# The expert weights of a mixture-of-experts decoder layer, asked for by GpSimd in its own DMA queue

## The chip, the core and the metric

The kernel runs on one core of one Trainium2 chip. The time is the device time of one execution in microseconds, as the median of several runs. All data are 32-bit floats.

## What is computed

Three blocks follow one another, each with a layer norm ahead and a residual addition behind: windowed attention, a long convolution against a context, and a feed-forward block. Only the last touches the change. It has a shared part and 64 experts; each of the 2048 tokens goes to 6 of them, and an expert takes at most 128:

```python
xd = zeros(E, CAP + 1, D).at[e_flat, slot].set(x[tok])        # E 64, CAP 128, D 512
h = square(relu(einsum('ecd,eid->eci', xd, w1)))              # I 256
yd = einsum('eci,edi->ecd', h, w2)
routed = zeros(T, D).at[tok].add(yd[e_flat, slot] * gate)     # T 2048
out = x + square(relu(x @ su.T)) @ sd.T + routed
```

## The kernel before

The kernel is written engine by engine, with semaphores between the engines. The attention and the convolution end at about 480 us; the router and the shared part follow, and from about 550 us to the end the kernel is the loop over experts.

For each expert four things move. The load brings its weights, 128 rows of 8 KB, 1 MB, from HBM into one of 8 slots (`wring`, four slots of their own, two in the upper half of the residual tile `X`, two below `xg`). The gather (`gather`, L592) brings the 128 token rows of 2304 B that the router chose, out of `token_rows` in HBM, into one of 8 slots of `xg`. TensorE transposes them (`tokens_T`, L1652), multiplies by the first weights (`hidden`, L1659) and by the second (`outputs`, L1669). VectorE scales the result by the gates into one of NY = 4 slots of `ysb` and writes the row numbers for GpSimd (L1334 to L1336). The scatter (`scatter`, L598) adds these 128 rows of 2 KB into `out` in HBM. Two experts may hold the same token, so a scatter waits until the one before has landed (`pool.wait_ge(added, before)`). After every 15 scatters of a group of 16, one scatter of 256 KB more (`scatter_tiles`, L611) adds a tile of the shared part, which TensorE computes between the experts; it stands in the same chain.

GpSimd's order for slot n is: wait for VectorE's rows, wait for scatter n-1 to land, scatter n, a product on one column (`begun_mark`, L609) that raises `scatter_begun`, gather n+8. The product stands behind the scatter on GpSimd and so tells SyncE that the scatter's descriptors have been written.

SyncE holds the loads (L414 to L434). Load n+6 waits for `scatter_begun` to pass n+1; the slot that it fills was last read by expert n-2. The first six loads wait for nothing of this kind: they follow the write of the gates (L413), the fifth and sixth also the write of the upper result rows (`upper_written`, L420). Between loads six and seven SyncE writes the lower result rows to HBM in three parts (L422 to L426), on which the first scatter waits.

SyncE's and ScalarE's transfers run in hardware queues (q1 and q10 in the profile), GpSimd's in a software queue (q0).

Of the kernel before, what the change touches and what calls it, by code (L numbers as in the profile page):

```python
# [6 lines left out]
P = 128  # L7
B, S, D = 8, 256, 512
T = B * S
# [10 lines left out]
E, K, NG, TKG, CAP, I = 64, 6, 8, 4, 128, 256  # L20
# [41 lines left out]
def program(nc, a, out):  # L62
    f32, u32 = mybir.dt.float32, mybir.dt.uint32
    ALU, ACT, AX = mybir.AluOpType, mybir.ActivationFunctionType, mybir.AxisListType
    V, G, A, TE = nc.vector, nc.gpsimd, nc.scalar, nc.tensor
    ds = bass.ds
# [6 lines left out]
    with ctx:  # L73
        def sb(name, shape, dt=f32):
            return ctx.enter_context(nc.sbuf_tensor(name, shape, dt))

        def sem(name):
            return ctx.enter_context(nc.semaphore(name))


        X = sb("residual", [P, NT, D])
# [9 lines left out]
        minus_half = sb("minus_half", [P, NT])  # L91
# [6 lines left out]
        idxs = sb("scatter_rows", [P, 4], u32)  # L98
        idxt = sb("tile_scatter_rows", [P, 1], u32)
        tile_rows = sb("tile_rows", [P, NT // 4])  # L100
        begun_mark = sb("begun_mark", [P, 1])
        AREA = 34400
        arena = sb("arena", [P, AREA])
        place = [0]
# [61 lines left out]
        NW, AHEAD = 8, 6  # L166
# [32 lines left out]
        UE, NY = 8, 4  # L199
# [18 lines left out]
        empt = [sem(f"bank{k}_drained") for k in range(NBANK)]  # L218
# [51 lines left out]
        tile_ready = sem("shared_tile_ready")  # L270
        added = sem("rows_added_to_the_result")
        scatter_landed = sem("scatter_landed")
        scatter_begun = sem("scatter_descriptors_written")
        out_written = sem("result_rows_begun")
        upper_written = sem("upper_result_rows_begun")

# [75 lines left out]
        FS = Fills(FC.after, names)  # L352
# [7 lines left out]
        @block.sync  # L360
        def _(sp):
            for u in range(4):
                sp.dma_start(X[:, u, :], a["x"][u * P:(u + 1) * P, :]).then_inc(tile_loaded[u], 16)

            def load(dst, name, s):
                sp.dma_start(dst, a[name]).then_inc(s, 16)

            load(wq, "wq", w_loaded)
            load(wkv, "wkv", w_loaded)
            load(rope, "rope", tables_loaded)  # L370
            load(bias, "bias", tables_loaded)
            load(bo, "bo", tables_loaded)
            load(wo, "wo", tables_loaded)
            load(kpad[:, P:], "kern", small_loaded)
            load(dcol[:], "skip", small_loaded)

            for s in (*empt, *conv_used, *conv_filled, *y_filled, *y_ready, hsq_ready, tile_ready):
                sp.sem_inc(s, 1)
            sp.sem_inc(scatter_landed, 5)
            sp.sem_inc(conv_done, 2)  # L380

            sp.wait_ge(tables_loaded, 16 * 4)
            for i in range(1, PAIRS):
                if i > 1:
                    sp.wait_ge(x_loaded, i * 16 - 16)
                sp.dma_start(X[:, i * 4:i * 4 + 4, :],
                             a["x"][i * (4 * P):(i + 1) * (4 * P), :].rearrange("(t p) d -> p t d", p=P)).then_inc(x_loaded, 16)

            sp.wait_ge(consts_ready, 1)
            sp.dma_start(out[T:ROWS, :], zeros[:]).then_inc(zero_written, 16)  # L390
            sp.dma_start(xrows[T:ROWS, 0:D], zeros[:]).then_inc(zero_written, 16)
            sp.dma_start(xrows[T:ROWS, D:XW], zeros[:, 0:E]).then_inc(zero_written, 16)
            sp.wait_ge(pad_ready, 1)
            sp.dma_start(toep[:], kpad[:]).then_inc(toep_written, 16)

            sp.wait_ge(full[FA1.bank(("vmid",))], FA1.filled(("vmid",)))
            sp.wait_ge(toep_written, 16)
            toep_v = bass.AP(toep.tensor, 1, [[P + D, SH], [1, P], [1, D]])
            with sp.Fori(0, SH // NTR) as i:
                for s in range(NTR):  # L400

                    sp.wait_ge(conv_filled[s], i + 1)
                    sp.wait_ge(toep_written, 16)
                    sp.dma_start(tring[:, s:s + 1, :], toep_v[ds(i * NTR + s, 1), :, :].rearrange("h p d -> p h d"))\
                      .then_inc(head_loaded[s], 16)
                    sp.dma_start(cring[:, s, :, :].rearrange("p m i -> p (m i)"),
                                 a["ctxE"][ds((i * NTR + s) * P, P), :]).then_inc(head_loaded[s], 16)

            for k, t in enumerate(TILES3):
                sp.wait_ge(x3_ready[k % NX], k // NX + 1)  # L410
                sp.dma_start(xrows[t * P:(t + 1) * P, 0:D], x3[:, k % NX, :]).then_inc(x3_written[k % NX], 16)
            sp.wait_ge(gates_ready, 1)
            sp.dma_start(xrows[0:T, D:XW].rearrange("(t p) c -> p t c", p=P), W).then_inc(gates_written, 16)  # L413
            def load_expert(s, i):  # L414
                sp.dma_start(wring[s], a["wexp"][ds((i * UE + s) * P, P), :]).then_inc(wexp_loaded[s], 16)

            for s in range(UE):
                if s == 4:

                    sp.wait_ge(upper_written, 16)  # L420
                if s == 6:
                    for first, last in ((0, 3), (4, 6), (7, 7)):  # L422
                        name = ("dn", last // 4, last % 4)
                        sp.wait_ge(empt[FS.bank(name)], FS.drained(name))
                        sp.dma_start(out[0:T, :].rearrange("(t p) d -> p t d", p=P)[:, first:last + 1, :],
                                     X[:, first:last + 1, :]).then_inc(out_written, 16)  # L426
                if s >= AHEAD:
                    sp.wait_ge(scatter_begun, s - AHEAD + 1)
                load_expert(s, 0)
            with sp.Fori(1, E // UE) as i:  # L430
                for s in range(UE):

                    sp.wait_ge(scatter_begun, i * UE + (s - AHEAD + 1))
                    load_expert(s, i)  # L434

            sp.wait_ge(added, 16 * (E + NT // 4))

# [2 lines left out]
        def _(pool):  # L440
# [142 lines left out]
            G.drain()  # L583
            G.tensor_scalar(W, W, 2.5, None, ALU.mult).then_inc(gates_ready, 1)

            for k in range(NX):
                pool.wait_ge(x3_written[k], 16 * (NT // NX))
            pool.wait_ge(gates_written, 16)
# [9 lines left out]
            def scatter(s, i, before):  # L598

                pool.wait_ge(y_ready[s % NY], i * (UE // NY) + (s // NY + 2))  # L600
                if before is not None:
                    pool.wait_ge(added, before)
                    pool.sem_inc(scatter_landed, 1)
                pool.indirect_dma_start(out, bass.IndirectOffsetOnAxis(ap=idxs[:, s % NY:s % NY + 1], axis=0),  # L604
                                        ysb[:, s % NY, :], None, compute_op=ALU.add).then_inc(added, 16)

                if before is not None:
                    pool.wait_ge(scatter_begun, i * UE + s)
                G.tensor_tensor(begun_mark[:], minus_half[:, 0:1], minus_half[:, 0:1], ALU.mult).then_inc(scatter_begun, 1)  # L609

            def scatter_tiles(j):  # L611
                pool.wait_ge(tile_ready, j + 2)
# [1174 lines left out]
```

## Time and profile before

| | us |
|---|---|
| median of 3 runs | 976.17 |
| lowest and highest | 974.54, 979.42 |
| the profiled execution | 984.94 |
| its span | 982.7 |
| TensorE busy | 895.9 |
| VectorE busy | 552.3 |
| GpSimd busy | 462.6 |
| ScalarE busy | 232.2 |
| moved by DMA | 143.40 MB |

The profiled execution is 8.8 us longer than the median. Its own time is 2.2 us more than its span. Times in the trace count from the span's start. "Busy" of GpSimd at a transfer is the time in which it writes the transfer's descriptors, not the time in which data move; the idle time in brackets stands ahead of an instruction, with what ended it. The shares of a DMA queue are the time that its packets took, over 16 engines and the stretch asked for. A link of the chain of scatters, as the word is used below, is the time from the start of one scatter on GpSimd to the start of the next.

### The profile page before, as it was taken

How to read it: one execution, taken by the hardware profiler on the slowest of the kernel's cores; microseconds unless marked ns; L12 is line 12 of the kernel's file. 1: busy time of each engine (PE TensorE's matmuls, PEld its weight loads, DVE VectorE, ACT ScalarE, POOL GpSimd, SP SyncE). 2: the span in 40 equal slices, each digit the busy share in tenths (PEclk: the TensorE clock that was granted, in tenths of full speed). 3: DMA queues.
4: the chain of work that ended last, by engine and by line, in shares of the span. 5: the costliest groups of instructions: out<-in, count | busy, mean ns of one | idle time of the engine just before them, and what ended most of it. 6: DMA issues, size and time to landing. Idle time of an engine off the chain costs nothing. (4 is left out here: it accounts for less than half of the span.)

```text
span 982.7 us, 14587 instructions
## 1 busy us (share of the span) xinstructions
PE 895.9 (91%) x4941; PEld 624.8 (64%) x4941; DVE 552.3 (56%) x1145; ACT 232.2 (24%) x715; POOL 462.6 (47%) x513
## 2 busy tenths in 40 slices
PE   5899999998999999999999999999999899989880
PEld 3666666665777777775444586867766667675640
DVE  4787888878688888977888323222222222212220
ACT  1555656462300000122100021211111111111110
POOL 1644352536488888620271344444444444444432
PEclk9989999999999999999999999999999999999995
DMA  7300000020633333042007568988898898888863
GB/s 293 113 1 2 1 2 1 2 76 1 236 93 93 93 94 93 1 150 108 1 1 275 180 197 259 268 257 225 254 274 261 226 265 254 261 241 247 236 148 53
DMA packets 44190, 143.40 MB, mean 146 GB/s; under 512 B 7345, under 2 KB 11697, under 8 KB 35185
## 3 DMA queue, kind: packets, MB, share of 16 engines
q1 hardware_dynamic: 27472, 98.56, 27.3%
q0 software_dynamic: 14912, 37.76, 19.6%
q10 hardware_dynamic: 1760, 6.49, 1.7%
q8 instruction: 27, 0.44, 0.2%
q14 instruction: 19, 0.15, 0.0%
HBM read 114.36 MB, written 28.43 MB: 145 GB/s over the span
## 5 line engine op out<-in xcount | busy, mean ns | idle before, releaser
L1375 PE MATMUL ps<-arena 128*128 128x128 f32 (+4 forms) x2112 | 511.2, 400 | 9.3 <-DVE arena L817 5.7
L1375 PEld LDWEIGHTS ps<-arena 128*128 128x128 f32 x2112 | 336.9, 191 | 146.6 <-issue 101.7
L604 POOL DMA_INDIRECT out<-arena,scatter_rows x64 | 101.2, 1581 | 219.0 <-DMA out<-arena,scatter_rows 145.4
L1309 DVE TENSOR_TENSOR arena<-arena 128x256 f32<-128x256 f32 x64 | 27.5, 430 | 219.8 <-ACT arena L802 213.5
L1375 PE MATMUL ps<-features_T,arena 128*128 (+2 forms) x640 | 116.0, 338 | 0.0
L1375 PEld LDWEIGHTS ps<-features_T,arena 128*128 128x128 f32 x640 | 84.7, 188 | 37.3 <-issue 37.3
L654 ACT ACTIVATE arena<-ps 128x512 f32<-128x512 f32 (+1 forms) x136 | 78.1, 591 | 117.5 <-PE ps L1656 49.0
L475 POOL TENSOR_TENSOR arena<-arena 128x512 f32<-128x512 f32 x48 | 49.3, 1060 | 89.6 <-DVE arena L837 89.6
L802 ACT ACTIVATE arena<-ps 128x256 f32<-128x256 f32 x64 | 24.6, 384 | 257.9 <-PE ps L1375 249.7
L593 POOL DMA_INDIRECT arena<-token_rows,gather_rows x64 | 66.1, 1034 | 38.2 <-DVE gather_rows L1302 27.1
L664 ACT ACTIVATE arena<-arena 128x128 f32<-128x128 f32 x192 | 74.0, 388 | 17.2 <-DVE arena L825 17.2
L528 POOL TENSOR_TENSOR arena<-arena 128x512 f32<-128x512 f32 x32 | 40.7, 1273 | 47.1 <-DVE arena L1094 47.1
L1656 PEld LDWEIGHTS ps<-ident,arena 128*128 128x128 f32 x256 | 30.1, 140 | 49.8 <-DMA arena<-token_rows,gather_rows 33.2
L1694 PE MATMUL ps<-arena 128*128 128x512 f32 x128 | 57.5, 592 | 0.0
L1656 PE MATMUL ps<-ident,arena 128*128 128x128 f32 x256 | 39.2, 276 | 20.1 <-DMA arena<-token_rows,gather_rows 20.1
L1334 DVE COPY scatter_rows<-slot_rows_u 128x1 uint32 (+1 forms) x64 | 9.8, 154 | 71.6 <-PE ps L1375 56.4
L609 POOL TENSOR_TENSOR begun_mark<-minus_half 128x1 f32<-128x1 f32 x64 | 50.0, 781 | 0.0
L1336 DVE TENSOR_SCALAR arena<-ps,arena 128x512 f32<-128x512 f32 x64 | 47.9, 748 | 0.0
L1694 PEld LDWEIGHTS ps<-arena 128*128 128x128 f32 x128 | 24.3, 190 | 30.6 <-issue 30.6
L765 ACT ACTIVATE arena<-features_T 128x256 f32 x32 | 13.0, 416 | 122.0 <-DVE arena L1094 120.2
L1101 DVE TENSOR_REDUCE arena<-arena 128x1024 f32 (+1 forms) x32 | 38.7, 1208 | 0.0
L664 ACT ACTIVATION_READ_ACCUMULATOR arena<-arena 128x1 f32 x192 | 36.1, 188 | 0.0
(178 smaller groups left out, 1086.8 us busy)
## 6 DMA issues: line engine op xcount, KB each, us to landing
arena<-wexp SPq DMA_DIRECT2D x48, 1024.0 KB
residual<-wexp SPq DMA_DIRECT2D x16, 1024.0 KB
arena<-toeplitz_rows SPq DMA_DIRECT2D x32, 256.0 KB, 3.1
arena<-ctxE SPq DMA_DIRECT2D x32, 192.0 KB, 3.2
token_rows<-arena SPq DMA_DIRECT2D x16, 256.0 KB, 2.4
residual<-x SPq DMA_DIRECT2D x3, 1024.0 KB, 5.3
arena<-suT ACTq DMA_DIRECT2D x1, 2048.0 KB, 7.7
arena<-sdT ACTq DMA_DIRECT2D x1, 2048.0 KB, 12.4
```

The lines of the kernel that those rows point to most:

```text
L475: G.tensor_tensor(e, e, rinv[:, b, 4 * c:4 * c + 4, q:q + 1].broadcast_to((P, 4, P)), ALU.mult)\
L528: G.tensor_tensor(halfsum[:, s % 2].rearrange("p m j k -> p (m j) k"), pv[:, :, 0:4], pv[:, :, 4:8], ALU.add).then_inc(half_ready, 1)
L593: pool.indirect_dma_start(xg[:, s, :], None, xrows, bass.IndirectOffsetOnAxis(ap=idxg[:, s:s + 1], axis=0))\
L604: pool.indirect_dma_start(out, bass.IndirectOffsetOnAxis(ap=idxs[:, s % NY:s % NY + 1], axis=0), ysb[:, s % NY, :], None, compute_op=ALU.a ...
L609: G.tensor_tensor(begun_mark[:], minus_half[:, 0:1], minus_half[:, 0:1], ALU.mult).then_inc(scatter_begun, 1)
L654: A.activation(dst, src, ACT.Copy, **kw).then_inc(empt[bank], 1)
L664: ins = A.activation(prob[:, b, k, q, :], prob[:, b, k, q, :], ACT.Exp, bias=negmax[:, b, k, q:q + 1], scale=1.0, accum_out=rowsum[:, b, k ...
L1101: V.tensor_reduce(o[:, 0:2 * B, :], prodb[:, s % 2, 0:2 * B], axis=AX.X, op=ALU.add)
L1336: V.tensor_scalar(ysb[:, s % NY, :], ps[:, 4 + s % 2, :], xg[:, s, ds(i * UE + (D + s), 1)], None, ALU.mult)\
L1375: ins = TE.matmul(out_ap, lhsT, rhs, start=(n == 0), stop=(n == len(pairs) - 1))
L1656: ins = TE.transpose(ps[:, bank, c * P:(c + 1) * P], xg[:, s, c * P:(c + 1) * P], ident[:])
L1694: ins = TE.matmul(ps[:, 7, :], htile[:, k, :], sdT[:, k, :], start=(k == 0), stop=(k == 7))
```

## The change

GpSimd issues the loads. The helper `load_expert` moves from SyncE to GpSimd, with the slot and the expert's number as arguments. GpSimd issues the first AHEAD = 6 loads after the last product on the gates and before it waits for the row numbers, with the wait on `upper_written` ahead of the fifth. After that, load n+6 follows scatter n directly and stands ahead of gather n+8. The one-column product, its tile, the semaphore `scatter_begun`, the wait on it and SyncE's loop are gone. SyncE keeps the three writes of the lower result rows. Slots, sizes, lead and the waits of all other engines stay.

```diff
@@ sync
-            def load_expert(s, i):
-                sp.dma_start(wring[s], a["wexp"][ds((i * UE + s) * P, P), :]).then_inc(wexp_loaded[s], 16)
-
-            for s in range(UE):
-                if s == 4:
-
-                    sp.wait_ge(upper_written, 16)
-                if s == 6:
-                    for first, last in ((0, 3), (4, 6), (7, 7)):
-                        name = ("dn", last // 4, last % 4)
-                        sp.wait_ge(empt[FS.bank(name)], FS.drained(name))
-                        sp.dma_start(out[0:T, :].rearrange("(t p) d -> p t d", p=P)[:, first:last + 1, :],
-                                     X[:, first:last + 1, :]).then_inc(out_written, 16)
-                if s >= AHEAD:
-                    sp.wait_ge(scatter_begun, s - AHEAD + 1)
-                load_expert(s, 0)
-            with sp.Fori(1, E // UE) as i:
-                for s in range(UE):
-
-                    sp.wait_ge(scatter_begun, i * UE + (s - AHEAD + 1))
-                    load_expert(s, i)
+
+            for first, last in ((0, 3), (4, 6), (7, 7)):
+                name = ("dn", last // 4, last % 4)
+                sp.wait_ge(empt[FS.bank(name)], FS.drained(name))
+                sp.dma_start(out[0:T, :].rearrange("(t p) d -> p t d", p=P)[:, first:last + 1, :],
+                             X[:, first:last + 1, :]).then_inc(out_written, 16)
@@ gpsimd, behind the last product on the gates
+            def load_expert(slot, ahead):
+                pool.dma_start(wring[slot], a["wexp"][ds(ahead * P, P), :]).then_inc(wexp_loaded[slot], 16)
+
+            for s in range(AHEAD):
+                if s == 4:
+                    pool.wait_ge(upper_written, 16)
+                load_expert(s, s)
+
@@ gpsimd, scatter(s, i, before)
-                if before is not None:
-                    pool.wait_ge(scatter_begun, i * UE + s)
-                G.tensor_tensor(begun_mark[:], minus_half[:, 0:1], minus_half[:, 0:1], ALU.mult).then_inc(scatter_begun, 1)
+                if not isinstance(i, int) or i * UE + s + AHEAD < E:
+                    load_expert((s + AHEAD) % UE, i * UE + (s + AHEAD))
```

## Rows read from the trace of the kernel before

**Rows 1.** Stages: stretch, length, busy us by engine, TensorE's clock, DMA share, GB/s.

```profile
569.00:636.00 67.00, 67.00 (x419) 51.30 (x418) 18.60 (x49) 13.02 (x28) 32.28 (x35) 1.00 0.86 255
636.00:955.00 319.00, 297.90 (x1694) 213.94 (x1692) 83.29 (x227) 50.94 (x111) 141.19 (x147) 0.99 0.85 244
```

**Rows 2.** Waits, 560 to 960 us: who waited for what, us, times, longest.

```profile
POOL out L604 <- DMA out<-arena,scatter_rows: 141.6, 46, 6.9
PEld ps L1656 <- DMA arena<-token_rows,gather_rows: 33.2, 20, 4.4
POOL out L604 <- DVE arena L1336: 20.8, 4, 11.2
```

**Rows 3.** Timeline of GpSimd, links of the chain of scatters: start, length, instruction, idle before.

```profile
633.93 1.58 POOL L604 DMA_INDIRECT out<-arena,scatter_rows  x1 [2.28 <-DMA out<-arena,scatter_rows]
...
643.85 1.58 POOL L604 DMA_INDIRECT out<-arena,scatter_rows  x1 [6.93 <-DMA out<-arena,scatter_rows]
644.88 0.77 POOL L609 TENSOR_TENSOR begun_mark<-minus_half 128x1 f32<-128x1 f32 x1
645.81 1.04 POOL L593 DMA_INDIRECT arena<-token_rows,gather_rows  x1 [0.16 <-issue]
649.24 1.58 POOL L604 DMA_INDIRECT out<-arena,scatter_rows  x1 [2.38 <-DMA out<-arena,scatter_rows]
...
930.99 1.58 POOL L604 DMA_INDIRECT out<-arena,scatter_rows  x1 [6.85 <-issue]
...
947.40 1.56 POOL L604 DMA_INDIRECT out<-arena,scatter_rows  x1 [3.76 <-DMA out<-arena,scatter_rows]
...
952.82 1.56 POOL L604 DMA_INDIRECT out<-arena,scatter_rows  x1 [3.55 <-DMA out<-arena,scatter_rows]
...
969.44 1.56 POOL L615 DMA_INDIRECT out<-arena,tile_scatter_rows  x1 [3.70 <-DMA out<-arena,scatter_rows]
976.25 1.55 POOL L604 DMA_INDIRECT out<-arena,scatter_rows  x1 [5.25 <-issue]
```

**Rows 4.** By line: VectorE's scaling, L1336, ns and first and last; scatters, L604, to landing.

```profile
L1336 DVE TENSOR_SCALAR arena<-ps,arena x64: 740/750/752, 567.7 to 955.3; 128x512 f32<-128x512 f32 x64
...
DMA to landing us min/median/max: 4.5/4.8/9.1
```

**Rows 5.** DMA queues in 649.24:654.79, 633.93:643.85, 947:969, 580:933, 550:557, in that order.

```profile
q0 software_dynamic: 224, 0.56, 50.1%
q1 hardware_dynamic: 147, 1.07, 46.3%
...
q1 hardware_dynamic: 252, 1.81, 47.8%
q0 software_dynamic: 303, 0.85, 38.3%
...
q0 software_dynamic: 576, 1.05, 37.9%
...
q0 software_dynamic: 12608, 31.96, 45.2%
q1 hardware_dynamic: 7865, 57.22, 41.3%
...
q0 software_dynamic: 372, 1.39, 75.5%
```

**Rows 6.** SyncE's issues of the loads: ns min/median/max, first and last.

```profile
L415 SPq DMA_DIRECT2D arena<-wexp x48: 332/333/1387, 521.5 to 938.4; - x48
```

**Rows 7.** GpSimd by line, 580 to 933 us: busy us, mean ns, idle before.

```profile
L593 POOL DMA_INDIRECT arena<-token_rows,gather_rows x55 | 57.2, 1041 | 8.8 <-issue 8.8
```

**Rows 8.** Timelines of GpSimd and of SyncE's queue at the loop's start.

```profile
518.30 2.80 POOL L584 TENSOR_SCALAR arena<-arena 128x1024 f32<-128x1024 f32 x1 [0.16 <-issue]
548.17 1.23 POOL L593 DMA_INDIRECT arena<-token_rows,gather_rows  x1 [27.07 <-DVE gather_rows L1302]
525.25 0.99 SPq L415 DMA_DIRECT2D residual<-wexp  x2
```

More of the change, by code:

```diff
@@ L100, in program @@
         tile_rows = sb("tile_rows", [P, NT // 4])
-        begun_mark = sb("begun_mark", [P, 1])
         AREA = 34400
@@ L272, in program @@
         scatter_landed = sem("scatter_landed")
-        scatter_begun = sem("scatter_descriptors_written")
         out_written = sem("result_rows_begun")
```

## The prediction

> **What bounds the kernel now.** I read the stages first, then the waits, then the single links of the chain. TensorE's busy share of the whole (895.9 of 982.7 us) names TensorE, but is an average. The table by stage [rows 1] splits the mixture-of-experts loop: from 569 to 636 us TensorE never stops, from 636 to 955 us it is busy 297.90 of 319.00 us, so it lacks 21.1 us; after 955 us the last scatters go on for 28 us without it. The waits [rows 2] say what it lacks: gathered token rows. The same table says what GpSimd, which asks for those rows, waits for: 141.6 us in 46 waits for its own last scatter to land, and 20.8 us in 4 waits for rows from VectorE. So from about 636 us the bound is a chain on GpSimd: a scatter-add may start only when the one before has landed. 64 expert scatters and 4 tile scatters make 67 links from 569.34 to 976.25 us, 406.9 us, 6.07 each.
>
> The timeline of GpSimd [rows 3] gives the link. Undisturbed it takes 643.85 to 649.24 = 5.39 us. Near the end, when no weights and no token rows are moved, it is the same: 947.40 to 952.82 = 5.42. A tile scatter makes 6.81. So 5.45 is the latency of one link and not a share of bandwidth, and the floor of the chain is 63 x 5.45 + 4 x 6.8 = 370.6 us. TensorE's own floor: the 64 products reach VectorE from 567.7 to 955.3 us [rows 4], 387.6 us, less the 21.1 us of idle: 366.5. The two nearly coincide, and the chain has 406.9 - 370.6 = 36.3 us above its floor. The longest links hold half of that. Five take more than 8 us; the first of them is 633.93 to 643.85 = 9.92 us, the last ends at 930.99 us after an idle time of 6.85 where an undisturbed link has 2.4 [rows 3]. Together they take 45.3 us against 27.3, 18 us of excess.
>
> What fills a long link is in the DMA table. In the link 649.24 to 654.79, near the floor, the transfers of q0 (GpSimd's) take 50.1% of the 16 engines and those of q1 (weights) 46.3%; in the long one q1 has 252 packets against 147 and 47.8%, beside q0's 38.3% [rows 5]; a scatter lands after 4.8 us in the median and 9.1 at most [rows 4]. Packets of the weights that were asked for after this scatter move while it is still unfinished.
>
> **What the change removes, adds and moves.** (1) SyncE's loop goes: its waits and issues of 333 ns [rows 6]. SyncE has nothing else to do there; worth nothing.
>
> (2) The one-column product goes with its wait: 0.77 us busy [rows 3]. In a link [rows 3] the scatter issues at 0, the product at 1.03, the gather at 1.96, and GpSimd is free at 3.00, then idle for 2.4 us until the landing. So it is hidden: nothing on the path.
>
> (3) In its place GpSimd issues the load, 128 rows of 8 KB. No row shows a plain transfer from GpSimd. The nearest are the gather, 128 rows in 1041 ns [rows 7], and the start of the product 1.03 us behind the scatter [rows 3]. From below: SyncE's 333 ns. From above: the scatter writes 128 pieces of 2 KB in 1.03 us; if a load's rows were cut to 2 KB too, it would be 512 pieces, 4.2 us. I take 1.04, the nearest in kind, plus an estimated 0.1 for the steps that form the address. The gather then starts at 1.03 + 1.14 = 2.2 instead of 1.96 and GpSimd is free at 3.2; the next scatter is due at 5.4. Cover 2.2 us: the sum is zero up to a load cost of about 3.4 us and each us above that is 1 us per link.
>
> (4) The start of the loop: GpSimd now asks for six loads after its last gate product, which ends at 521.1, and then waits for the row numbers until 548.17, 27 us idle [rows 8]. Six times 1.14 us fit. SyncE gave loads five and six out at 525.25 [rows 8], so the wait on the upper rows' write that now stands on GpSimd was over by then; behind it in the queue are only waits that end at 548. Nothing. SyncE's three writes of result rows wait for nothing new.
>
> (5) The order of the transfers. This is where the time can move. Today q0 holds scatter n, gather n, scatter n+1, and q1 the loads; on an engine that is late they share. Now one queue holds scatter n, load n, gather n, scatter n+1. The work of each, from [rows 5]: four scatters alone take 37.9% of 22 us, 2.08 us each on all engines; in 580 to 933 us q1's 57.22 MB, 54.6 loads, take 41.3% of 353 us, 2.67 us each; q0's 45.2% is 159.6 us, less 55 x 2.08 and three tile scatters of twice that, leaves 32.7 us, 0.6 per gather. Sum 5.35 us, against a link of 5.45: it just fits. The link 649.24 to 654.79 has 50.1% + 46.3% [rows 5], so there is a little room and no more. Load n is ready directly behind scatter n instead of after GpSimd's mark, SyncE's wake-up and issue, and fills it earlier.
>
> The gain: in a long link the late engine must no longer carry load n (2.67 us) and its share of gather n before it finishes scatter n; it must carry what was left of load n-1, which it carries now too. I take 2.0 us of the 3.6 us excess of each of the five long links, 10 us, and 0.05 us of each of some 45 other expert links after 636 us, 2 us: 12 us. Not more, because the same stall holds every engine in either order, and because up to 636 us TensorE sets the pace. TensorE lacks 21.1 us, so it can follow the 12. 982.7 - 12 = 970.7 for the span, 973 for this execution's 984.94. The median of the runs shown is 976.17, 8.8 us less than the profiled execution, so the excess without the profiler is about 27 instead of 36 us; the gain scales to 9: **967 us**.
>
> The Trainium skill (DMA: Bandwidth & Descriptors, Queues, rings and completion order) says that each engine takes turns between queues packet by packet, and works off one queue in order. That is the mechanism behind the gain, and the long link's two shares [rows 5] agree.
>
> **The rivals.** *A, the forecast:* 967, own range 955 to 974.
>
> *B, no change:* the long links come from stalls that hold all packets alike, so order is worth nothing. For it: in the long link q0 and q1 together fill 86% of the engines against 96% in the good one [rows 5], so part of it is no question of turns. Against: q1's extra packets in it. 976, range 972 to 980.
>
> *C, slower:* loads can no longer be put off. Today they have six experts of lead and the scatter takes its turn beside what is left of them; in one queue scatter n+1 stands behind all of load n and gather n. It decides where the work of a link exceeds 5.45 us, and I have 5.35, on an edge: 10% on a load (2.94) already gives 5.6. I price it at 0.35 us per link on the 50 links after 636 us, +17: 993. For it: the DMA shares are near full, and six gathers right after one another in 550 to 557 us, 1.39 MB, took 75.5% of 7 us, 3.8 us for a MB where q1 needs 2.55 [rows 5]; a load at that price is 4.0 us, a link 6.7. Against: that stretch starts on idle engines. Between scatters a gather comes out at 0.6 us for 0.29 MB, about q1's rate, and a load will stand behind a scatter in the same way. So I keep 2.67 for the forecast and 0.35 for C.
>
> *D, issue cost:* the load costs 4.2 us on GpSimd (512 pieces); 0.8 above the cover on 60 links, +50: 1026. Against: 64 gathers of 128 rows at 1041 ns.
>
> *E, slow transfers from GpSimd:* a load moves at the rate of all that q0 moves. 159.6 us for 31.96 MB [rows 5] is 5.0 us for a MB, 5.2 a load; a link is then 2.08 + 5.2 + 0.6 = 7.9, 1.8 above today's 6.07 on some 58 links, +105: 1081. Against: the scatters are most of those 159.6 us, and a scatter both reads and adds. The Trainium skill (DMA: Bandwidth & Descriptors, Bandwidth) gives 6.15 us for a 1 MB load issued from GpSimd; by that the kernel would end near 1135. Its section SWDGE vs HWDGE vs iDMA has plain transfers issued from SyncE or ScalarE, a rule against this change. No row here shows a load from GpSimd.
>
> **How the numbers follow.** A 0.42, B 0.20, C 0.25, D 0.07, E 0.06. Faster or slower by over 0.5% (4.9 us, about what a measurement of this kernel can tell from no change) means below 971.3 or above 981.1. A gives 0.40 of faster and 0.02 of same; B 0.02 of faster, 0.16 of same, 0.02 of slower; C 0.04 of same and 0.21 of slower; D and E slower. Faster 0.42, same 0.22, slower 0.36. The range leaves out D, E and the outer tails of A and C, together under 0.2: 952 to 1000. Both signs are well populated, so A's own range, 955 to 974, is the one to read beside it.
>
> **What the profile of the changed kernel would show.** Right: links over 8 us gone or under 7.5; undisturbed links at 5.4 to 5.5; the load's instruction near 1.0 us on GpSimd and still over 1.5 us of idle before each scatter; TensorE's waits for gathers below 10 us; hardly any traffic on q1 after 570 us. C would show undisturbed links of 5.7 and more, with a scatter that lands after more than 5.0 us. D would show GpSimd's scatter waiting for issue and not for a landing; E a link near 8 us. The prediction fails most easily if a load from GpSimd takes the engines longer than q1's 2.67 us, since the sum 5.35 has 0.1 us to spare.

## The result, and the profile after

The changed kernel takes 1007.53 us in the median of 4 runs (1006.98 to 1009.09), the kernel before 977.79 us beside it. The ratio on record is 1.0315, 95% interval 1.0274 to 1.0356 (the two medians alone give 1.0304): about 30 us slower, where 9 us faster was forecast. The profiled execution took 1006.98 us with a span of 1004.9 us. Of the four runs of e13 below, two were in a slower state of the chip, and its time and ratio are those of the two fast ones.

The first view is the table by stage of the changed kernel; its columns are those of [rows 1].

```profile
569.00:636.00 67.00, 67.00 (x424) 51.86 (x424) 19.04 (x50) 12.84 (x28) 32.66 (x30) 1.00 0.84 235
636.00:955.00 319.00, 287.03 (x1619) 212.81 (x1618) 77.96 (x213) 48.96 (x107) 158.30 (x145) 0.95 0.86 241
955.00:1005.00 50.00, 19.35 (x83) 11.32 (x81) 6.12 (x18) 2.14 (x6) 13.12 (x9) 0.73 0.45 76
```

Up to 636 us nothing has changed for TensorE: it never stops. From 636 to 955 us it lacks 32.0 us where it lacked 21.1 [rows 1], and it still has 19.35 us of work after 955 us, where it had none. The DMA engines are as full as before (0.86 against 0.85) but move 241 GB/s against 244. TensorE's granted clock falls as well, from 0.99 to 0.95, in the stretch in which it has more idle time.

The waits from 560 to 990 us say for what, and are the rows that answer [rows 2]:

```profile
POOL out L595 <- DMA out<-arena,scatter_rows: 141.2, 49, 4.6
PEld ps L1646 <- DMA arena<-token_rows,gather_rows: 40.1, 19, 6.2
PE ps L1646 <- DMA arena<-token_rows,gather_rows: 32.0, 13, 6.0
POOL out L595 <- DVE arena L1326: 11.4, 1, 11.4
```

The bound is the same chain. GpSimd waits for a scatter to land and hardly ever for data: VectorE's rows are waited for once instead of four times, 11.4 us instead of 20.8, so it isn't a slower TensorE or VectorE that holds the chain up. The 67 links now run from 570.46 to 995.33 us, 424.9 instead of 406.9 us. The profiled executions differ by 22 us, 18 of them in the chain; that of the kernel before was itself 7 us above its median, so the medians differ by 30.

The timeline of GpSimd shows two kinds of link, the answer to [rows 3]. (Start, length, instruction; the idle time ahead of it in brackets.)

```profile
703.61 1.62 POOL L595 DMA_INDIRECT out<-arena,scatter_rows  x1 [3.87 <-DMA out<-arena,scatter_rows]
704.63 1.21 POOL L570 DMA_DIRECT2D arena<-wexp  x1
709.24 1.62 POOL L595 DMA_INDIRECT out<-arena,scatter_rows  x1 [2.09 <-DMA out<-arena,scatter_rows]
710.26 1.22 POOL L570 DMA_DIRECT2D arena<-wexp  x1
716.74 1.62 POOL L595 DMA_INDIRECT out<-arena,scatter_rows  x1 [3.95 <-DMA out<-arena,scatter_rows]
```

The load stands 1.02 us behind the scatter and takes 1.21 us; GpSimd is idle for 2.1 us even in the short link (5.63 us) and for almost 4 us in the long one (7.50). Taking the difference of each two scatter starts in this view: the median of the 63 links that start with an expert scatter is 5.86 us, before it was 5.64. Among them links over 8 us went from 5 to 2 (8.17 and 8.13), but links over 6.5 us went from 11 to 20. The five very long ones were traded for many of 7 to 7.8 us, 14 instead of 1. (Of the four links behind tile scatters, one grew from 6.65 to 8.66 us.)

By line, the scatters and the loads of the changed kernel, and under each the time from issue to landing (compare [rows 4] for the scatters):

```profile
L595 POOL DMA_INDIRECT out<-arena,scatter_rows x64: 1551/1617/2130, 570.5 to 995.3; - x64
...
DMA to landing us min/median/max: 4.6/5.0/7.4
...
L570 POOL DMA_DIRECT2D arena<-wexp x48: 550/1211/1250, 522.2 to 956.0; - x48
...
DMA to landing us min/median/max: 6.4/8.8/18.1
```

The DMA queues tell the rest. First both kernels in the same stretch, 650 to 900 us (q0 and q1 of the kernel before, then q0 of the changed one), then loads alone: the kernel before in 530 to 538 us and the changed one in 528 to 534 us. Columns: packets, MB, share of the 16 engines.

```profile
q0 software_dynamic: 9000, 22.98, 46.4%
q1 hardware_dynamic: 5501, 39.96, 40.3%
```

```profile
q0 software_dynamic: 13653, 59.30, 85.5%
```

```profile
q1 hardware_dynamic: 479, 3.43, 101.8%
```

```profile
q0 software_dynamic: 361, 2.58, 101.9%
```

Alone, loads from GpSimd are as quick as loads from SyncE: 1.019 x 6 us / 2.58 MB = 2.37 us for a MB, and 1.018 x 8 / 3.43 = 2.37. Between scatters and gathers they are not. Before, the packets took 0.867 x 250 / 62.94 MB = 3.44 us of all engines for a MB; after, 0.855 x 250 / 59.30 = 3.60 us. An expert moves 1.64 MB (load 1.05, gather 0.29, scatter 0.26, its part of the tile 0.03), so its packets take 5.91 instead of 5.64 us. I call this the packet time of an expert below. (The prediction's sum of 5.35 us is the same quantity without the tile scatters, which it left out.) It is made of the times that packets take, so a packet that only waits in its engine counts too. It is therefore partly an effect of the order of the transfers and not a pure price of the load: the experiments give it between 5.68 and 6.13 us with the same whole loads from GpSimd.

### The profile page after: what moved, and what is told of

It is laid out like the page before. It is cut to its first block and busy times, and to the rows that moved or that the text cites. A ratio compares the mean times of both kernels' runs of the same rounds, so it can differ in the third digit from the quotient of the medians.

```text
span 1004.9 us, 14411 instructions
## 1 busy us (share of the span) xinstructions
PE 903.9 (90%) x4941; PEld 634.4 (63%) x4941; DVE 552.1 (55%) x1145; ACT 232.1 (23%) x715; POOL 489.3 (49%) x513
## 5 line engine op out<-in xcount | busy, mean ns | idle before, releaser
L1365 PE MATMUL ps<-arena 128*128 128x128 f32 (+4 forms) x2112 | 519.8, 406 | 8.7 <-DVE arena L807 5.7
L1365 PEld LDWEIGHTS ps<-arena 128*128 128x128 f32 x2112 | 345.3, 197 | 146.0 <-issue 101.3
L595 POOL DMA_INDIRECT out<-arena,scatter_rows x64 | 103.7, 1621 | 204.9 <-DMA out<-arena,scatter_rows 141.2
L584 POOL DMA_INDIRECT arena<-token_rows,gather_rows x64 | 65.8, 1028 | 42.4 <-DVE gather_rows L1292 23.6
L1646 PE MATMUL ps<-ident,arena 128*128 128x128 f32 x256 | 41.4, 287 | 32.0 <-DMA arena<-token_rows,gather_rows 32.0
L1646 PEld LDWEIGHTS ps<-ident,arena 128*128 128x128 f32 x256 | 31.8, 146 | 60.6 <-DMA arena<-token_rows,gather_rows 40.1
L570 POOL DMA_DIRECT2D arena<-wexp x48 | 55.8, 1162 | 0.0
L1684 PEld LDWEIGHTS ps<-arena 128*128 128x128 f32 x128 | 24.4, 191 | 30.5 <-issue 30.5
```

The costliest lines, as they stand in the source:

```text
L570: pool.dma_start(wring[slot], a["wexp"][ds(ahead * P, P), :]).then_inc(wexp_loaded[slot], 16)
L584: pool.indirect_dma_start(xg[:, s, :], None, xrows, bass.IndirectOffsetOnAxis(ap=idxg[:, s:s + 1], axis=0))\
L1365: ins = TE.matmul(out_ap, lhsT, rhs, start=(n == 0), stop=(n == len(pairs) - 1))
L1646: ins = TE.transpose(ps[:, bank, c * P:(c + 1) * P], xg[:, s, c * P:(c + 1) * P], ident[:])
L1684: ins = TE.matmul(ps[:, 7, :], htile[:, k, :], sdT[:, k, :], start=(k == 0), stop=(k == 7))
```

## The experiments

Three theories stand against one another. **W**: what the packets of an expert take on the engines sets the time, and loads from GpSimd take more. **Q**: the single queue has a price of its own, because a scatter stands behind everything that was put in before it. **P**: GpSimd's own time for issuing the loads is what costs. G, S and "sharing" name smaller rivals where they come up. "Packet time" is worked out for each run as above, from its DMA queues in 650 to 900 us. For cut loads the MB of an expert are fewer. "Chain" is the time from the first scatter to the last in the profiled execution. The ratio compares with runs of the kernel before from the same series, whose medians lie between 976.4 and 982.8 us; it is the ratio on record and need not be the quotient of two medians.

| kernel | total us | ratio to before (95%) | chain us | packet time us |
|---|---|---|---|---|
| before | 977.79 | | 406.9 | 5.64 |
| changed | 1007.53 | 1.0315 (1.0274 to 1.0356) | 424.9 | 5.91 |
| e1 gather ahead of load | 1013.32 | 1.036 (1.0296 to 1.0424) | 432.7 | 6.13 |
| e2 load ahead of scatter | 1071.47 | 1.0955 (1.087 to 1.1039) | 490.7 | 5.68 |
| e3 changed, half loads | 963.14 | 0.9847 (0.9774 to 0.9921) | 382.8 | 4.72 |
| e4 before, half loads | 959.11 | 0.9806 (0.9731 to 0.9881) | 381.5 | 4.46 |
| e5 loads from both | 1019.52 | 1.0431 (1.0342 to 1.052) | 438.0 | 5.93 |
| e6 before, loads in two parts | 991.62 | 1.0144 (1.006 to 1.0228) | 413.4 | 5.91 |
| e7 load after landing | 1018.92 | 1.0399 (1.0296 to 1.0502) | 438.8 | 5.74 |
| e8 changed, product back | 1008.28 | 1.0291 (1.0194 to 1.0388) | 429.5 | 5.98 |
| e9 changed, 1856 columns | 992.17 | 1.0154 (1.0101 to 1.0207) | 412.4 | 5.71 |
| e10 before, 1856 columns | 967.93 | 0.9928 (0.989 to 0.9966) | 386.7 | 5.39 |
| e11 changed, 1664 columns | 979.15 | 1.0025 (0.9991 to 1.0059) | 395.8 | 5.43 |
| e12 before, 1664 columns | 963.58 | 0.9868 (0.9803 to 0.9933) | 386.8 | 5.20 |
| e13 pairs from SyncE | 1036.04 | 1.056 (quotient of the medians) | 458.6 | 5.48 |
| e14 pairs from GpSimd | 1083.65 | 1.1026 (1.0988 to 1.1065) | 503.8 | 5.83 |

### Is it the bytes in the queue, or the issue on GpSimd? Half the load (e3, e4)

```diff
- pool.dma_start(wring[slot], a["wexp"][ds(ahead * P, P), :])
+ pool.dma_start(wring[slot][:, 0:1024], a["wexp"][ds(ahead * P, P), 0:1024])
```

(e4 has the same edit in SyncE's loop. The first six loads stay whole.)

> The changed kernel whose loads from the seventh on bring only the first 4 KB of each row, the first part of the first weights; the rest of the slot keeps the weights of an earlier expert. GpSimd issues as many loads as before. Theory Q: the queue's work per link falls from about 5.5 to 4.2 us, below the latency of 5.45, so the links go to 5.4 to 5.5 us, none but a few above 6.5, and TensorE becomes the bound: total 950 to 962. Theory P (issue or path): the number of loads and their issue are the same, so the links stay above 5.7 and the total above 990.

> The kernel before with the same halved loads from the seventh on, from SyncE. Theory Q: with half the bytes neither order has a full engine, so it comes to the same time as the changed kernel with halved loads within 5 us, 950 to 962. Theory P: it is ahead of it by about the 25 us that separate the two full kernels.

Measured: 963.1 and 959.1 us, 4 us apart as Q has it, with e3 1 us above its range. The median link is 5.60 us in e3 and 5.58 in e4, and TensorE is busy 290 and 289 of the 294 us from 636 to 930, so it sets part of the pace now. The number of loads is the same as in the full kernels, the issue of a half load on GpSimd takes 1.21 us like that of a whole one, and the gap falls from 30 to 4 us. P, with links above 5.7 us and a total above 990, is out: what costs goes with the bytes. The engines are no longer full; q0 of e3 in 650 to 900 us:

```profile
q0 software_dynamic: 15510, 45.89, 77.8%
```

The packet time of an expert is 4.72 us in e3 and 4.46 in e4. The surplus of loads from GpSimd, 0.26 us, is there in full, just as with whole loads (0.27), but it costs nearly nothing: a link of 5.45 us has room for it. In these runs packet time counts only where it comes near the latency of a link.

### Is issuing really covered? (e8)

```diff
+ G.tensor_tensor(begun_mark[:], minus_half[:, 0:1], minus_half[:, 0:1], ALU.mult).then_inc(scatter_begun, 1)
  if not isinstance(i, int) or i * UE + s + AHEAD < E:
      load_expert((s + AHEAD) % UE, i * UE + (s + AHEAD))
```

> The changed kernel with the one-column product and its wait back between the scatter and the load: GpSimd's own work per link grows by 0.8 to 0.9 us. Theory Q: GpSimd is idle for over 2 us ahead of each scatter, so the issue is hidden; the load and the gather reach the queue 0.9 us later, which costs nothing as long as the scatter still moves then: 1007 within 6 us. Theory P (GpSimd's issue time is the cost): 0.8 us per link more, 1050.

Measured 1008.3 us, no change. (Its profiled execution has a chain 4.7 us longer than the changed kernel's, a median link of 6.17 us and 26 links over 6.5. Counts of links in one execution can differ that much between kernels of equal time.) The run tests less than it was meant to: the timeline shows the load starting while the product runs.

```profile
704.48 1.62 POOL L597 DMA_INDIRECT out<-arena,scatter_rows  x1 [1.94 <-DMA out<-arena,scatter_rows]
705.52 0.80 POOL L602 TENSOR_TENSOR begun_mark<-minus_half 128x1 f32<-128x1 f32 x1
705.66 1.22 POOL L572 DMA_DIRECT2D arena<-wexp  x1
707.17 1.03 POOL L586 DMA_INDIRECT arena<-token_rows,gather_rows  x1 [0.30 <-issue]
711.96 1.63 POOL L597 DMA_INDIRECT out<-arena,scatter_rows  x1 [3.76 <-DMA out<-arena,scatter_rows]
```

The gather starts 2.69 us behind the scatter; in the changed kernel the load alone puts it at 2.5. So GpSimd's work grew by about 0.2 us and not by 0.8 to 0.9. The result agrees with a hidden issue; the proof of that is in e3.

### Do late gathers cost? (e1)

```diff
# in outline
  scatter(n)
- load(n + 6)
  gather(n + 8)
+ load(n + 6)
```

> The changed kernel with gather and load in the other order: scatter n, gather n+8, load n+6. Theory Q (one queue: a scatter waits for all that was put into the queue before it, so every delay of a load reaches the chain): load and gather both still stand ahead of the next scatter, so the chain keeps its time, 424.9 us for 67 links within 6 us, and the total stays near 1007; TensorE's waits for gathers get shorter by a few us because the gathers land up to 2.7 us sooner. Theory G (the loss comes from gathers that land late behind the loads, and the chain only follows TensorE): the total returns to 980 to 990.

Measured 1013.3 us, a little more than the changed kernel. TensorE's waits, 560 to 1000 us:

```profile
PE ps L1371 <- issue: 27.9, 20, 3.5
PEld ps L1652 <- DMA arena<-token_rows,gather_rows: 10.2, 5, 3.2
PE ps L1652 <- DMA arena<-token_rows,gather_rows: 8.4, 3, 3.0
```

The waits for gathers fall from 32.0 and 40.1 us to 8.4 and 10.2, and the time does not fall at all; the idle time turns up at the products instead (27.9 us, where the kernel waits for a free row buffer or bank). G is refuted: gathers that land sooner don't bring the time back. Q was right about the gathers and a little off on the chain: 432.7 us where 424.9 within 6 was expected. The packet time rises too, to 6.13 us, with nothing but the order changed. Why the order gather, load is slightly worse was not settled.

### What a load directly ahead costs, in the same queue and in another (e2, e7)

```diff
  pool.wait_ge(added, before)
+ load_expert((s + AHEAD) % UE, i * UE + (s + AHEAD))        # e2
  pool.indirect_dma_start(out, ..., compute_op=ALU.add).then_inc(added, 16)
- load_expert((s + AHEAD) % UE, i * UE + (s + AHEAD))
```

```diff
- sp.wait_ge(scatter_begun, i * UE + (s - AHEAD + 1))        # e7, SyncE, from the kernel before
+ sp.wait_ge(added, 16 * (n + n // GROUP))                   # n = expert - AHEAD + 1
```

> The changed kernel with load n+6 issued directly ahead of scatter n, behind the wait for the landing of scatter n-1. Theory Q: the scatter now stands behind a whole fresh load, so a link grows from about 5.8 by the load's 2.7 us of transfer to 8 to 8.5 us, the total to 1140 to 1180. Theory P (what costs is the issue of the load on GpSimd, 1.2 us, and not the queue): a link grows by the issue alone, 1.2 us, total about 1080. If order in the queue meant nothing and issue were hidden: 1007.

> The kernel before without the one-column product: SyncE gives out load n+6 when scatter n has landed, about 3 us later than before, so that its packets move together with those of scatter n+1 in another queue. Theory Q: even then the two queues share, and a link stays shorter than in the run with the load directly ahead of the scatter in one queue (7.45 us): 6 to 6.8 us, total 985 to 1030. If sharing between queues gave the scatter nothing, 7.2 us or more and 1050 or more. If the time of the load did not matter at all: 978.

Measured: e2 1071.5 us, e7 1018.9 us. The link of e2, from its timeline:

```profile
652.28 0.56 POOL L570 DMA_DIRECT2D arena<-wexp  x1 [3.64 <-DMA out<-arena,scatter_rows]
653.14 1.63 POOL L597 DMA_INDIRECT out<-arena,scatter_rows  x1 [0.31 <-issue]
655.07 1.01 POOL L584 DMA_INDIRECT arena<-token_rows,gather_rows  x1 [0.30 <-issue]
659.72 0.57 POOL L570 DMA_DIRECT2D arena<-wexp  x1 [3.63 <-DMA out<-arena,scatter_rows]
660.59 1.63 POOL L597 DMA_INDIRECT out<-arena,scatter_rows  x1 [0.30 <-issue]
```

A link is 7.45 us: 0.87 us of issue ahead of the scatter, and a landing after 5.9 us in the median instead of 5.0. Q had 8 to 8.5 us and 1140 to 1180 in total and is too high; it counted the whole load. P's 1080 is nearer, and rightly so here: ahead of the scatter the issue can't be hidden and makes 0.87 of the 1.6 us by which the link grew. That Q's part is smaller than a load may come from the load starting to move before the scatter's own packets are ready, which no view here shows. e7 came out where Q had it: a link of 6.5 us, 1019 us in total. Its landing takes 5.7 us (e2 first):

```profile
DMA to landing us min/median/max: 4.5/5.9/7.3
```

```profile
DMA to landing us min/median/max: 4.5/5.7/7.5
```

In e7 SyncE gives the load out 0.77 us ahead of the scatter (at 653.85 us, the scatter starts at 654.62), in e2 GpSimd does so 0.86 us ahead; in the kernel before it is 1.98 us behind. So at about the same lead a load in another queue holds a scatter up almost as long as one in the scatter's own queue, and the difference of the two totals is mostly the 0.87 us of issue. A second queue is weaker protection than I had taken it for. What counts here is how much of a load has been given out when the scatter comes.

### How much is packet time, how much the single queue? (e6, e9 to e12)

e6 gives the kernel before the packet time of the changed one by other means: SyncE asks for each load in two parts. (TensorE's wait on the load, not shown, counts both.)

```diff
- sp.dma_start(wring[s], a["wexp"][ds((i * UE + s) * P, P), :]).then_inc(wexp_loaded[s], 16)
+ for h in (0, 1024):
+     sp.dma_start(wring[s][:, h:h + 1024], a["wexp"][ds((i * UE + s) * P, P), h:h + 1024]).then_inc(wexp_loaded[s], 16)
```

> The kernel before with each load as two transfers from SyncE of 128 rows of 4 KB, one after the other, both behind the same product. Theory Q with turns taken between the two queues: smaller packets of the loads give the scatter its turn sooner on an engine that is late, so the links above 6.5 us get shorter, total 968 to 976. If turns do not matter: 978 within 4 us; if the larger number of packets costs: 980 to 985.

Measured 991.6 us, ratio 1.0144: 14 us slower, above all three expected ranges. My hope that finer packets give the scatter its turn sooner is refuted; it became a control instead. Its queues in 650 to 900 us:

```profile
q0 software_dynamic: 8731, 22.24, 45.0%
q1 hardware_dynamic: 10650, 38.77, 43.0%
```

0.88 x 250 / 61.01 MB = 3.61 us for a MB, 5.91 us for an expert, the same as the changed kernel, with the loads still in SyncE's queue. At this packet time SyncE's queue gives 1.0144 and GpSimd's 1.0315.

The other way round, the loads of both kernels are cut by 9% and by 19%:

```diff
- pool.dma_start(wring[slot], a["wexp"][ds(ahead * P, P), :])
+ pool.dma_start(wring[slot][:, 0:1856], a["wexp"][ds(ahead * P, P), 0:1856])     # e9; e11: 1664
```

> The changed kernel whose loads from the seventh on bring 1856 of 2048 columns of each row, 9% less; the last columns of the second weights stay those of an earlier expert. Theory W (a load from GpSimd costs the 16 engines some 0.25 us more per expert, 3.6 against 3.4 us for a MB of all traffic, and the engines are full): 9% of a load is 0.25 us, so it comes back to the kernel before, 974 to 982. Theory Q (the single queue has a price of its own, because the scatter cannot take its turn when an engine is late): it stays above, 984 to 996.

> The kernel before with the same cut of the loads, from SyncE. The engines are at their limit in the kernel before too, so 0.25 us less work per link gives 0.15 to 0.25 us per link back: 964 to 970. If the kernel before had slack in its engines: 976 to 980, no change.

> The changed kernel with loads of 1664 of 2048 columns, 19% less. Theory W: the time of the kernel before with 1856 columns, 964 to 970. Theory Q: 970 to 980, since the engines are late less often but the order still costs when they are.

> The kernel before with loads of 1664 of 2048 columns. Both theories: near the floor that halved loads gave (959), 958 to 965.

Measured: 992.2, 967.9, 979.2 and 963.6 us. The queues in 650 to 900 us, e9 and then e10:

```profile
q0 software_dynamic: 14154, 57.82, 85.8%
```

```profile
q0 software_dynamic: 9479, 24.17, 49.6%
q1 hardware_dynamic: 5808, 38.25, 37.8%
```

Q's ranges hold in e9 and e11, W's in neither; e10 and e12 came out as expected. The gap between the two kernels goes 30, 24, 16, 4 us with 2048, 1856, 1664 and 1024 columns. Two pairs stand at nearly the same packet time: e9 (5.71) has 992 us and the kernel before (5.64) 977.8; e11 (5.43) has 979.2 and e10 (5.39) 967.9. From before to e10, 0.25 us of packet time are 7 us by the ratio and 10 by the medians, so the small differences explain 3 and 2 us at most of the 14 and 11. Some 9 to 11 us stay with the single queue there. At full size it is about 17, by 1.0315 against 1.0144; with intervals of 0.4% and 0.8% that is 17 within about 9. The rest of the 30 us, about 13, goes with the packet time. Both theories are needed, and the runs can't fix their shares closely. That the two parts simply add is an assumption. So is their being separate: with whole loads from GpSimd the packet time is 5.68 us in e2, 5.91 in the changed kernel, 5.98 in e8 and 6.13 in e1, so the order moves it as well.

The cut of the kernel before is also worth a look: 9% fewer bytes in the loads gave 0.7% of the time, twice as much cut gave 1.3%. Some of the time of the kernel before goes with the bytes already.

### A longer burst ahead of every second scatter (e13, e14)

```diff
+ wpair = [wfixed[:, 0:2, :], wfixed[:, 2:4, :], whigh, wlow]
- sp.dma_start(wring[s], a["wexp"][ds((i * UE + s) * P, P), :]).then_inc(wexp_loaded[s], 16)
+ sp.dma_start(wpair[s // 2], a["wexp"][ds((i * UE + s) * P, 2 * P), :].rearrange("(k p) n -> p k n", p=P))
+   .then_inc(wexp_loaded[s], 16)                              # even s alone; e14 the same from GpSimd
```

(TensorE waits for the load of the pair, not shown.)

> The kernel before with one transfer of 2 MB for two experts, given out by SyncE after every even scatter; the slots allow it. Same bytes, half as many load transfers. Theory W (what the engines work per MB sets the time): half the transfers cost less, some 3.37 us for a MB instead of 3.44; if the engines stay as full, 966 to 974. Theory Q (order): the second half of the 5.3 us burst moves together with the next scatter, from another queue, so it delays it by less than its own length: odd links 6.5 to 7, even ones 5.4, total 975 to 995.

> The changed kernel with one transfer of 2 MB for two experts, given out by GpSimd behind every even scatter. Theory W alone: fewer transfers, so it gains on the changed kernel as the SyncE version gains on the kernel before, 995 to 1003, and the two pair versions lie 25 to 31 us apart. Theory Q: the odd scatter stands behind the whole burst and a gather in one queue, 2.08 + 5.3 + 0.6 = 8 us for that link, and 5.4 for the other: mean 6.8 to 7, total 1035 to 1055, so the two pair versions lie 50 us or more apart.

Measured: 1036.0 and 1083.7 us, 48 us apart, near the 50 of Q and far from the 25 to 31 of W. As totals both theories missed: Q had 975 to 995 and 1035 to 1055, W less. The packets get cheaper, as W says (5.48 and 5.83 us for an expert), and both kernels get much slower, so packet time doesn't set the time here. The timeline of e14 shows the price of order most plainly:

```profile
699.56 1.58 POOL L597 DMA_INDIRECT out<-arena,scatter_rows  x1 [2.41 <-DMA out<-arena,scatter_rows]
700.57 1.40 POOL L571 DMA_DIRECT2D arena<-wexp  x1
...
705.24 1.62 POOL L597 DMA_INDIRECT out<-arena,scatter_rows  x1 [1.97 <-DMA out<-arena,scatter_rows]
...
715.58 1.59 POOL L597 DMA_INDIRECT out<-arena,scatter_rows  x1 [7.41 <-DMA out<-arena,scatter_rows]
716.60 1.38 POOL L571 DMA_DIRECT2D arena<-wexp  x1
```

The scatter with the burst behind it needs 5.68 us, the next, with the burst and a gather ahead of it in the queue, 10.34. Over the whole run links of even scatters have a median of 5.56 us, those of odd ones 9.93. Q's sum of 8 was too low. With the burst in SyncE's queue (e13) the links are not spared either; four scatters in a row from its timeline

```profile
701.26 1.58 POOL L606 DMA_INDIRECT out<-arena,scatter_rows  x1 [2.64 <-DMA out<-arena,scatter_rows]
709.08 1.58 POOL L606 DMA_INDIRECT out<-arena,scatter_rows  x1 [4.83 <-DMA out<-arena,scatter_rows]
714.38 1.65 POOL L606 DMA_INDIRECT out<-arena,scatter_rows  x1 [2.31 <-DMA out<-arena,scatter_rows]
723.91 1.58 POOL L606 DMA_INDIRECT out<-arena,scatter_rows  x1 [6.46 <-DMA out<-arena,scatter_rows]
```

make links of 7.82, 5.30 and 9.53 us; the medians are 5.52 us behind even and 7.82 behind odd scatters, where Q had 5.4 and 6.5 to 7.

### Loads from both engines (e5)

```diff
- load_expert((s + AHEAD) % UE, i * UE + (s + AHEAD))          # GpSimd, every slot
+ if s % 2: the one-column product, and SyncE loads slot s + 6  # odd slots
+ else:     pool.dma_start(...) of slot s + 6                   # even slots
```

> Loads of even slots from GpSimd directly behind the scatter as in the changed kernel, loads of odd slots from SyncE behind the one-column product as in the kernel before; both kinds in one run under the same conditions. Theory Q (the next scatter waits in the queue for everything ahead of it): a scatter that follows a load from GpSimd lands later than one that follows a load from SyncE; links that begin with a GpSimd load have a median of 5.8 to 5.9 us, the others 5.6 to 5.7, and the total lies between the two kernels, 988 to 998. Theory S (the changed kernel is slower for another reason, such as SyncE's loop or the start): no difference between the two kinds of link.

Measured 1019.5 us, slower than either kernel, which no theory had. Its packet time (5.93) is that of the changed kernel, but the engines are less full, 65.6% + 17.6% = 83.2% in 650 to 900 us. The timeline of GpSimd shows both kinds of link. A scatter followed by the product (L617) is odd, one followed by the load (L620) is even:

```profile
699.81 1.62 POOL L612 DMA_INDIRECT out<-arena,scatter_rows  x1 [2.01 <-DMA out<-arena,scatter_rows]
700.84 0.81 POOL L617 TENSOR_TENSOR begun_mark<-minus_half 128x1 f32<-128x1 f32 x1
...
708.36 1.59 POOL L612 DMA_INDIRECT out<-arena,scatter_rows  x1 [5.53 <-DMA out<-arena,scatter_rows]
709.39 1.21 POOL L620 DMA_DIRECT2D arena<-wexp  x1
...
713.99 1.61 POOL L612 DMA_INDIRECT out<-arena,scatter_rows  x1 [2.07 <-DMA out<-arena,scatter_rows]
...
720.34 1.76 POOL L612 DMA_INDIRECT out<-arena,scatter_rows  x1 [3.33 <-DMA out<-arena,scatter_rows]
```

The odd links here take 8.55 and 6.35 us, the even one between them 5.63. With the scatters numbered by their expert, the 32 links of even scatters have a median of 5.63 us and none is over 6.5; the 31 of odd scatters have 7.19 us and 20 are over 6.5. My expectation named the wrong link: by Q the late scatter is the one that stands behind a GpSimd load in the queue, and that is the odd one. It is late, by 1.6 us, so S, with no difference, is refuted.

The run also speaks against a rival that has no run of its own. The changed kernel gives a load out 1.02 us behind the scatter and the kernel before 1.98 us behind it, and this earlier start could be the cost (e8 moved it by 0.16 us only). Here the even scatters have a load 1.03 us behind them too, and they are not late.

Why the mixture is worse than both of its parts isn't tested. The odd scatter has a GpSimd load ahead of it in its own queue and a load from SyncE 2.0 us behind it in the other queue, and the second doesn't have to wait for its turn in the first queue. In the changed kernel (median link 5.86 us) both stand in one queue. This would explain it, but it stays a guess.

## Why the prediction was wrong, point by point

**The bound: right.** The chain of scatters stayed the bound, and its latency floor too: links without loads or gathers take 5.4 to 5.6 us in both kernels. Only with cut loads does TensorE come near its own limit (busy 290 of 294 us in e3).

**(1), (2), SyncE's loop and the product are worth nothing: agreed with.** Nothing waits on either after the change, and with the product back (e8) the time is the same.

**(3), the issue: right.** Forecast 1.14 us, measured 1.21, and GpSimd idle for about 2.1 us ahead of a scatter in undisturbed links. 512 pieces and rival D did not happen. The gather starts at 2.5 instead of the forecast 2.2 us.

**(4), the start of the loop: right.** The six loads are out within 3.5 us of 522.19, and the first gather starts at 549.24 against 548.17 us, after 23.6 us of idle time.

**(5), the order of the transfers: this step failed, in two terms.** The first is the price of a load. I took 2.67 us from q1's rows for a load from GpSimd, with the sum at 5.35 against a link of 5.45, and wrote that it had 0.1 us to spare. With the loads in GpSimd's queue the packet time of an expert rose by 0.27 us between scatters and gathers, though alone they are as fast as SyncE's. The edge was named and the sum set on its safe side, with the argument that gathers from GpSimd were cheap; that argument was worked out by subtraction and could not carry 0.1 us. The sum also left out the tile scatters, some 0.2 us per expert by its own figures (three of twice 2.08 us in 55 experts), though the measured packet time of the kernel before, 5.64 us, is still under the 406.9 / 64 = 6.36 us that an expert has in the chain.

The second is the gain. Only what the order does for the five longest links was counted. They did go, 5 to 2, so the mechanism exists. But a scatter now also has to wait for whatever of load n-1 and gather n-1 is left over, and at engines about 86% full something is left over often: links over 6.5 us went from 11 to 20 and the median link from 5.64 to 5.86. e5 shows it within one run, 7.19 us behind a GpSimd load against 5.63. I wrote of what was left of load n-1 that the late engine "carries now too"; by e9, e11 and e6 it costs some 10 to 17 us more in the single queue.

**The signs.** The forecast's own signs failed: two links over 8 us and many over 7.5 remained, and TensorE's waits for gathers came to 32.0 and 40.1 us, not under 10. C's came out about as written: short links mostly at 5.6 to 5.9 us, and a scatter that lands after 5.0 us in the median instead of 4.8.

**The rivals.** What happened is rival C, the one on the other side. Its mechanism and its place were right, its size was not: 0.35 us per link and 993 us, where the medians differ by 30 / 67 = 0.44 us per link over the whole chain. The range was drawn up to 1000 on it, 7.5 us short. A C of two terms, one for packet time and one of the same size for order, would have covered it. B did not happen, and E is refuted by the loads alone (2.37 us for a MB). The Trainium skill (DMA: Bandwidth & Descriptors, Bandwidth) gives 6.15 us for a 1 MB load from GpSimd. As a load's share of the engines, which is how rival E used it, the trace disagrees: such loads, one behind another, moved at 430 GB/s here, about 2.4 us each. From issue to landing a load took 6.4 us at least. The rule of the same page (SWDGE vs HWDGE vs iDMA) that plain transfers belong on SyncE or ScalarE agrees with the result, which came out 3.15% on its side.

**The state of the kernel before.** The forecast scaled its gain to the median, since the profiled execution was longer. Part of the long links, which carry most of the assumed gain, may belong to that one execution; the other executions were not profiled for it, so this stays a guess.

No version in these runs beats the kernel before with its full work.

## What to carry to other kernels

When a chain of dependent transfers sets the time, keep its own queue free of bulk transfers that are not urgent: here what stood in the queue ahead of a scatter made it late once the engines were some 86% full, though the weights were asked for six experts ahead of their use. When the sum of the transfers of one step lies within a few per cent of its latency, treat the kernel as bound by both, and price a move of any transfer at its unfavourable bound and not at the middle. Cutting the bytes of the suspect in both kernels is the experiment that tells issue cost from queueing: the gap closed from 30 to 4 us with the same number of issues.

## What the runs showed of the hardware that was not expected

- A 1 MB load of 128 rows costs the engines the same from GpSimd as from SyncE when loads follow one another (2.37 us for a MB each). Between scatters and gathers the packet time of an expert was 0.26 to 0.27 us higher with the loads behind the scatter in GpSimd's queue, with whole and with half loads alike; with the load ahead of the scatter (e2) it was 5.68 us, about that of the kernel before. Splitting SyncE's load in two adds the same 0.27 us; joining two in one takes 0.16 us off (5.64 to 5.48).
- A load given out 0.8 us ahead of a scatter in another queue held it up nearly as long as one 0.9 us ahead in the same queue: the scatter landed after 5.7 us (e7) and 5.9 us (e2), against 4.8 where the load came 1.98 us behind it (before).
- With loads from both queues (e5) a scatter behind a GpSimd load made a link of 7.19 us in the median, a scatter behind a SyncE load one of 5.63.
- GpSimd needs 0.55 to 0.6 us to issue a 1 MB load when it has nothing in front of it, and 1.21 us directly behind a scatter, which itself takes 1.6 us on GpSimd.
- Asking for 2 MB every second expert instead of 1 MB every one costs 5.6% from SyncE and 10.3% from GpSimd against the kernel before, with fewer transfers and 0.16 and 0.08 us less packet time than the same kernels with single loads.
